# One statistics instruction for two tiles read in turns, and the variance made by GpSimd, in a six-layer attention and expert kernel

## The reference

```python
def _layernorm(x, w, b):
    m = jnp.mean(x, axis=-1, keepdims=True)
    v = jnp.mean(jnp.square(x - m), axis=-1, keepdims=True)
    return (x - m) * jax.lax.rsqrt(v + LN_EPS) * w + b
...
for i in range(DEPTH):                       # 6 layers
    xn = _layernorm(x, ln1_w[i], ln1_b[i])
    q, k, v = ...                            # xn @ wq, wk, wv, 8 heads of 16
    attn = _linear_attn(q, k, v)             # softmax of q over features, of k over tokens
    x = attn @ wo[i] + bo[i] + x
    xn = _layernorm(x, ln2_w[i], ln2_b[i])
    hdn = xn @ w1[i]                         # 128 -> 512
    hdn = jnp.where(hdn >= 0, hdn, LEAKY_SLOPE * hdn)
    x = hdn @ w2[i] + x                      # 512 -> 128
```

## Time and profile before

| | |
|---|---|
| time, median of 3 runs | 596.95 us (596.15 to 597.39) |
| span of the profiled execution, first to last instruction | 594.9 us |
| median of the runs less that span | 2.05 us |
| TensorE busy | 578.7 us (97%) |
| VectorE busy | 540.1 us (91%) |
| ScalarE busy | 434.8 us (73%) |
| GpSimd busy | 311.1 us (52%) |
| mean granted clock of TensorE | 0.994 of full speed |

### The profile page before, as it was taken

How to read it: one execution, slowest core, us unless ns; L and a number is a source line. 1 busy time by engine, 2 the same in 40 slices (tenths; PEclk the granted TensorE clock), 3 DMA queues, 4 the chain that set the end, 5 groups by cost and what they waited for, 6 DMA issues and landing times.

```text
span 594.9 us, 12614 instructions
## 1 busy us (share of the span) xinstructions
PE 578.7 (97%) x4166; PEld 516.3 (87%) x4166; DVE 540.1 (91%) x1352; ACT 434.8 (73%) x763; POOL 311.1 (52%) x308
## 2 busy tenths in 40 slices
PE   7999999999999999999999999999999999999897
PEld 7899897887978889889889898898898898898796
DVE  6887999999988999999999999999999999988865
ACT  2658595876976868868768768768779678687652
POOL 5896134755852772442442532433523766867752
PEclk9989999999999999999999999999999999999999
DMA  8209233323224154445435435445342351441102
GB/s 282 75 10 328 72 110 121 124 94 130 95 84 152 71 152 146 112 133 169 124 123 163 109 141 150 116 163 158 103 165 80 108 167 57 129 156 62 45 36 106
DMA packets 74946, 73.20 MB, mean 123 GB/s; under 512 B 27265, under 2 KB 65153, under 8 KB 74882
## 3 DMA queue, kind: packets, MB, share of 16 engines
q1 hardware_dynamic: 72400, 68.18, 35.6%
q0 software_dynamic: 2048, 4.20, 2.3%
q10 hardware_dynamic: 434, 0.02, 0.0%
HBM read 39.87 MB, written 32.51 MB: 122 GB/s over the span
## 4 chain that ended last, share of the span: by engine, by line
PE 75%; DVE 11%; DMA 4%; issue 3%; POOL 3%; ACT 2%; SPq 1%; DVEq 0%; ACTq 0%; POOLq 0%
PE psY L513 23%; PE psH L406 6%; PE psS L558 6%; PE psH L407 6%; PE psH L408 6%; PE psT L592 6%; PE psT L401 6%; PE psT L526 5%; PE psM L538 5%; DVE st L1295 2%; PE psS L455 2%; DMA through<-blocks 1%; DVE X L1563 1%; DVE hid L1553 1%; DMA turned<-through 1%
## 5 line engine op out<-in xcount | busy, mean ns | idle before, releaser
L513 PE MATMUL psY<-w_all,hid 128*128 128x128 f32 x1536 | 188.7, 276 | 2.5 <-DVE hid L1553 1.8
L513 PEld LDWEIGHTS psY<-w_all,hid 128*128 128x128 f32 x1536 | 182.0, 193 | 6.6 <-issue 2.3
L1553 DVE TENSOR_TENSOR hid<-psH,hsl 128x512 f32<-128x512 f32 x192 | 127.2, 676 | 13.6 <-ACT hsl L936 13.1
L936 ACT ACTIVATE hsl<-psH 128x512 f32<-128x512 f32 x192 | 108.3, 591 | 42.0 <-PE psH L408 38.5
L2038 POOL TENSOR_TENSOR rstd<-veps,minus_half 128x8 f32<-128x8 f32 x44 | 72.7, 1653 | 61.2 <-DVE veps L1312 61.0
L2134 POOL TENSOR_TENSOR qsm<-qe,qrec 128x1024 f32<-128x1024 f32 x24 | 46.5, 1938 | 97.8 <-DVE qrec L1636 97.8
L2112 POOL TENSOR_TENSOR xn_lo<-xn,xn_hi 128x512 fp32r<-128x512 f32 x48 | 60.6, 1282 | 69.4 <-ACT xn_hi L1000 69.4
L406 PE MATMUL psH<-xn_hi,w_hi 128*128 128x512 f32 x192 | 86.4, 450 | 3.7 <-DVE hid L1553 3.4
L966 ACT ACTIVATE xh<-X,shift,rstd 128x128 f32<-128x128 f32 x188 | 77.0, 482 | 8.9 <-POOL shift L2041 8.7
L408 PE MATMUL psH<-xn_lo,w_hi 128*128 128x512 f32 x192 | 76.1, 396 | 0.0
L407 PE MATMUL psH<-xn_hi,w_lo 128*128 128x512 f32 x192 | 76.0, 396 | 0.0
(11 more groups left out here) (161 smaller groups left out, 1024.9 us busy)
## 6 DMA issues: line engine op xcount, KB each, us to landing
through<-turn SPq DMA_DIRECT2D x22, 512.0 KB, 2.7
turn<-through SPq DMA_DIRECT2D x88, 128.0 KB
through<-blocks SPq DMA_DIRECT2D x20, 512.0 KB, 3.2
turned<-through SPq DMA_DIRECT2D x80, 128.0 KB, 2.8
wb<-expert_rows SPq DMA_DIRECT2D x40, 128.0 KB, 2.0
sorted_x<-blocks SPq DMA_DIRECT2D x5, 512.0 KB, 4.4
xs_xsT<-sorted_x SPq DMA_DIRECT2D x40, 64.0 KB, 2.5
sorted_y<-ys SPq DMA_DIRECT2D x10, 256.0 KB, 2.4
```

Source lines behind the costliest of these rows:

```text
L513: last = nc.tensor.matmul(tile(psY, t), tile(hid[:, c, :], t), w2_all[:, n // NBATCH, c, :], start=(c == 0 and t == 0), stop=(c == NC - 1) ...
L936: nc.scalar.activation(hsl[:, i % 2, :], psH[:, i % 2, :], ACT.Copy, scale=SLOPE) \
L1553: nc.vector.tensor_tensor(hid[:, i % NC, :], psH[:, i % 2, :], hsl[:, i % 2, :], ALU.max) \
```

## The change

Two neighbouring tiles are read by one statistics instruction, element 0 of the first, element 0 of the second, element 1 of the first, and so on. The even places are then the first tile and the odd places the second, so the six numbers are already the statistics of two whole tiles. Nothing is left to join. There are four statistics instructions of 256 columns for a norm in place of eight of 128. The seven small VectorE instructions of a norm go; GpSimd makes variance plus epsilon and the negated mean with two instructions of its own ahead of the power. For the input the nine small VectorE instructions become three, which stay on VectorE. statistics1 and statistics2 now wait, ahead of their first statistics, until the shift of the norm before is made, since GpSimd reads st.

```diff
-        st = sb("st", [P, NORMS, NT, 6])
-        sdiff = sb("sdiff", [P, NORMS, NT])
-        sdev = sb("sdev", [P, NORMS, NT])
+        st = sb("st", [P, NORMS, NT // 2, 6])
...
+        def two_in_turn(a):
+            return a.rearrange("p (t d) -> p d t", t=2)
+
+        def by_tile_of_pair(norm):
+            return st[:, norm, :, :].rearrange("p a (k f) -> p (a k) f", f=3)
+
+        def tile_means(norm):
+            return by_tile_of_pair(norm)[:, :, 1]
+
+        def tile_squares(norm):
+            return by_tile_of_pair(norm)[:, :, 2]
...
-            def tile_statistics(norm, name, src, tiles=range(NT)):
-
-                for t in tiles:
-                    last = nc.vector.bn_stats(st[:, norm, t, :], src(t))
-                last.then_inc(sig(name + "_st"), 1)
-
-            def token_statistics(norm, name, st_count, count):
...
+            def pair_statistics(norm, src, b, pairs):
+
+                for k in pairs:
+                    last = nc.vector.bn_stats(st[:, norm, k, :], two_in_turn(xb(src, b, 2 * k * P, 2 * P)))
+                return last
...
-                for t in range(NT):
-                    last = nc.vector.bn_stats(st[:, k, t, :], xb(xraw, b, t * P, P))
-                last.then_inc(sig("in_st"), 1)
+                pair_statistics(k, xraw, b, range(NT // 2)).then_inc(sig("in_st"), 1)
                 dve.wait_ge(sig("in_st"), b + 1)
...
+                nc.vector.tensor_scalar(both_var[:, b, :], tile_squares(k), (1.0 + EPS) / D, EPS * EPS,
+                                        ALU.mult, ALU.add)
+                nc.vector.tensor_scalar(negmean[:, k, :], tile_means(k), -1.0, None, ALU.mult)
+                nc.vector.tensor_scalar(veps[:, k, :], tile_squares(k), 1.0 / D, EPS, ALU.mult, ALU.add) \
+                    .then_inc(sig("in_var"), 1)
...
                     dve.wait_ge(sig("x1_added"), n + 1)
-                    tile_statistics(1, "ln2", lambda t: xb(X, n % NBATCH, t * P, P))
                     wait(dve, "ln2_shift", n)
-                    token_statistics(1, "ln2", n + 1, n + 1)
+                    pair_statistics(1, X, n % NBATCH, range(NT // 2)).then_inc(sig("ln2_st"), 1)
...
                     wait(dve, "y_added", 2 * (n - NBATCH) + half + 1)
-                    norm1_half(n % NBATCH, half)
...
+                    wait(dve, "ln1_shift", turned_before1(n))
+                    pair_statistics(0, X, n % NBATCH, range(2 * half, 2 * half + 2)).then_inc(sig("ln1_st"), 1)
...
-            def reciprocal_deviations(norm, name, count):
-
+            def reciprocal_deviations(norm, name, count, st_count):
+
+                pool.wait_ge(sig(name + "_st"), st_count)
+                nc.gpsimd.tensor_scalar(veps[:, norm, :], tile_squares(norm), 1.0 / D, EPS, ALU.mult, ALU.add) \
+                    .then_inc(sig(name + "_var"), 1)
+                nc.gpsimd.tensor_scalar(negmean[:, norm, :], tile_means(norm), -1.0, 1.0, ALU.mult, ALU.mult) \
+                    .then_inc(sig(name + "_mean"), 1)
                 pool.wait_ge(sig(name + "_var"), count)
                 nc.gpsimd.tensor_tensor(rstd[:, norm, :], veps[:, norm, :], minus_half[:, :], ALU.pow) \
                     .then_inc(sig(name + "_rstd"), 1)
+                pool.wait_ge(sig(name + "_mean"), count)
                 pool.wait_ge(sig(name + "_rstd"), count)
```

More of the change, by code:

```diff
@@ L1494, in expert_bias @@
                                         ALU.add).then_inc(sig("ys_ready"), 1)
-            def norm1_half(batch, half):
-                tile_statistics(0, "ln1", lambda t: xb(X, batch, t * P, P), range(4 * half, 4 * half + 4))
             def stage_w1(l):
@@ L1577, in statistics1 @@
                     wait(dve, "y_added", 2 * (n - NBATCH) + half + 1)
-                    norm1_half(n % NBATCH, half)
-            def variances1(n):
-                if there(n) and n >= NBATCH:
-                    k = turned_before1(n)
-                    wait(dve, "ln1_shift", k)
-                    token_statistics(0, "ln1", 2 * k + 2, k + 1)
+                    wait(dve, "ln1_shift", turned_before1(n))
+                    pair_statistics(0, X, n % NBATCH, range(2 * half, 2 * half + 2)).then_inc(sig("ln1_st"), 1)
             def blocks_of_norm1(n):
@@ L1754, in _ @@
             output_bias(3)
-            variances1(4)
             blocks_of_norm2(2)
@@ L1780, in _ @@
             leaky(2, 0)
-            variances1(5)
             leaky(2, 1)
@@ L1807, in _ @@
             value_bias(5)
-            variances1(6)
             leaky(3, 2)
@@ L1835, in _ @@
             statistics1(7, 1)
-            variances1(7)
             leaky(4, 0)
@@ L1856, in _ @@
             statistics1(8, 1)
-            variances1(8)
             add_attention(6)
@@ L1885, in _ @@
             leaky(6, 0)
-            variances1(9)
             leaky(6, 1)
@@ L1915, in slot @@
                 leaky(s - 3, 0)
-                variances1(s)
                 key_maxima(s - 1)
@@ L2118, in deviations2 @@
                     wait(pool, "xh2_ready", 4 * n)
-                    reciprocal_deviations(1, "ln2", n + 1)
+                    reciprocal_deviations(1, "ln2", n + 1, n + 1)
             def deviations1(n):
@@ L2126, in deviations1 @@
                         pool.wait_ge(sig("xh1_ready"), xh1_parts(n - 1))
-                    reciprocal_deviations(0, "ln1", k + 1)
+                    reciprocal_deviations(0, "ln1", k + 1, 2 * k + 2)
             def scale_queries(n):
```

28 lines of the change are left out of this document (removed).

## The result

The changed kernel took 592.72 us (median; 592.33 to 593.05) where the kernel before took 597.1 beside it: ratio 0.9926, 95% interval 0.9913 to 0.9939. Two further series on the same day gave 0.9936 (0.9902 to 0.9969) and 0.9964 (0.9944 to 0.9983). The mean of the three ratios, 0.9942, is 3.5 us. The profiled execution took 592.57 with a span of 590.8, 4.1 us shorter than the 594.9 before.

What follows compares the result with a forecast made beforehand. TensorE bounds the kernel, so freed VectorE time pays only where VectorE ends TensorE's wait behind statistics. Terms -1.0 - 1.9 - 3.4 + 0.4 = -5.9 us gave 591.0 us; range 585.6 to 596.0, the forecast's own 587.5 to 593.5.

Steps and rivals of the forecast that it cites:

- Prices: Unit costs: 412 ns for a 256-column statistics instruction, 0.2 us for each small GpSimd one; VectorE busy near 475 us.
- The rival of dear reading: Reading two tiles in turns takes 0.6 us a statistics instruction, so the kernel takes around 593.2 us; chance 0.08.
- Start: Input norms: statistics finish 1.1 us sooner, and TensorE's 1.04 us hole at 11.74 closes; -1.0 us.
- Middle: TensorE's holes at 94.79, 171.87 and 202.17, 2.9 us together, close by two thirds; -1.9 us.
- Regular middle: Regular slots gain nothing, since TensorE is busy for 20.00 of 20 us there; 0.
- Gather slots: Slots 21 to 23: GpSimd is the late engine and its added instructions lengthen the chain, about 0.15 us each; +0.4 us.
- the last sentence of the prediction: Signs of being wrong, among them xnT coming later in the gather slots by more than some tenths of a us.
- End: Last norm2: hid starts 3.3 us earlier, closing the 1.76 us hole and removing 1.64 us of clock loss; -3.4 us.
- Its sign, hid within 1.5 us of the first statistics: Check at the end: hid of the last norm2 starts within 1.5 us of that norm's first statistics.
- The holes move: TensorE meets the next late producer each time, leaving a small gain, 593.5 to 595.7 us; chance 0.13.
- Slower through GpSimd: Gather slots: GpSimd's two additions at 1.65 us each would make +12, 609 us; chance 0.07.

Runs made afterwards that it cites:

- more on GpSimd: Changed kernel with four further 8-column tensor_scalars a norm on GpSimd, into an unread buffer: 603.37 us, ratio 1.0131 to the kernel before.
- small ones on VectorE: Changed kernel, but VectorE makes the layer norms' variance plus epsilon and negated mean: 591.71 us, ratio 0.9913 to before; second run 592.12, 0.9938.

## Why the prediction was right, and by how much it was off

The direction and the place of the gains held; the forecast was 1.7 us below the first median, and the gain forecast (5.9) is above the 3.5 of three series. The median lies in the forecast's range, and part of how near it came is luck: the first series' four runs of the changed kernel lost 0.3 us each to low clock, those of the two later series 1.7 and 1.8. With the low-clock windows taken out, and the two executions of before against the three of the changed kernel, the table gives it term by term.

*Prices.* Right: 418 ns and 202 ns. Four statistics take 1.43 us, not 1.32, which was four steps of 0.33; three steps and the full length of the last, as the eight were counted, make 1.40. VectorE's busy time is 487.5 where 475 was forecast, 52.6 saved instead of 65; 4.8 of the difference are those 0.11 us in 44 norms, the rest wasn't traced. The rival of dear reading falls. The Trainium skill's figure for a source that hops at every element (page "Vector Engine (DVE) Microarchitecture Reference", section "Measured stream behaviour on trn2") would give some 590 ns, an estimate; the measured 418 ns contradict it for a statistics instruction over two tiles in turns. What the same section of the Trainium skill says of a one-source stream that alternates between regions, full rate, agrees with the 418 ns.

*Start, -1.0.* Right: 0.3 at number 67 and 0.9 more up to 301, 1.2. The hole is gone, both_shift starts at 8.29 (8.2 forecast), and VectorE's first normalised half at 8.77. But TensorE was still in its warm-up matmuls until 11.43 (11.03 and 12.15 in the other two executions), where the kernel before had ended them at 10.59 and 11.21, so most of the gain shows behind them. The hole's size is no fixed quantity either: 1.04 in one execution of the kernel before, 0.56 in the other.

*Middle, -1.9.* Right in sum: 180.6 to 178.5, 2.1. The hole at 94.79 went and one of 0.62 for xnT came 2.6 us behind it (in the third execution it is the other way round, 0.74 at 94.47 and none for xnT); 1.24 at 171.87 became 0.71; 0.94 at 202.17 went.

*Regular middle, 0.* Right in effect: 245.5 and 245.6 on average. It isn't the balance of a full TensorE, though: with xnT in time it takes 244.6. How often it doesn't come in time changes with the execution, in either kernel.

*Gather slots, +0.4.* Under-sized: 79.7 to 80.6, +0.8. These slots begin earlier by the lead and run into xnT, as the last sentence of the prediction has it. GpSimd's own share can't be told apart from the scatter here.

*End, -3.4.* The step that failed, in both its parts. (Its sign, hid within 1.5 us of the first statistics, failed too: it took 2.8, 1.37 of them waiting for ScalarE, but that was early enough for the hole to close.) "With the hole gone I expect most of the clock loss gone as well", 1.64 us, fell with the second execution of the kernel before (same hole, no window) and with the means of all runs, 1.3 us lost before and 1.5 after. And the 1.76 came out, 17.52 to 15.58, but with it the normalising instructions came 5 us earlier (564.14, once 569.18) and met GpSimd's addition: 1.08 lost. The prediction saw that GpSimd's power would come late there and called it covered; it looked for the instructions behind it in the queue of VectorE, not at what would run on GpSimd beside them. By the means of the executions that makes -1.9 and +1.1, -0.8 in all.

Sum: -1.2 - 2.1 + 0.1 + 0.8 - 0.8 = -3.2 us, near the 3.5 of the ratios.

*The rivals.* "The holes move" described the middle's mechanism rightly: TensorE does meet the next late producer, which there is mostly xnT. "Slower through GpSimd" was far off at 202 ns an instruction, but its price was too low: it counted the three gather slots alone. By it, 0.64 us a norm would be 3 x 2 x 0.64 = 3.8 us, near the 3.5 of the gather slots in "more on GpSimd"; in all it was 9.3, as the first slots wait as well. The sum gave the two small instructions +0.4 in the gather slots; by the two runs of "small ones on VectorE" the move to GpSimd costs 1.3, 0.6 of it at the end.

## What to carry to other kernels

A freed engine's time is worth only what the next late producer lets through: before trusting a gain, follow that producer's chain to something that the change shortens, or find that nothing does. The same trace reads differently for more work than for less: 52 us fewer on VectorE brought 3.5, about as many more, in the same place, cost 10 to 12, and 28 more on GpSimd cost 9, both with ScalarE waiting some 18 and 13 us longer for shift. Of a change in two parts each part wants its own run: here the move to GpSimd costs 1.3 us of what the paired statistics bring. And when an edit starts an instruction earlier, read what the engine that shares its path is doing at the new time, and take from no single execution a clock window as a property of the program: the mean clock of many runs tells what the windows are worth.

## What the runs showed of the hardware

- One-input VectorE instructions wait too. The first normalising tensor_scalar at 564.14 (128 columns, one tensor from SBUF) took 1,783 ns, 334 in the others, and ended at 565.92, 0.08 behind GpSimd's addition. In all nine executions in which it met that addition it took 1,165 to 2,385 ns and ended 0.08 to 0.09 behind it; where it didn't, 336 to 339. A negated mean of 8 columns (L1313) took up to 1,890: in the second run of "small ones on VectorE" 20 of the 44 took over 400 ns, and 19 of these end 0.02 to 0.04 us behind an addition or product of GpSimd. So the engines don't meet only in semaphores. The prediction had taken only instructions with two SBUF inputs for this kind. The Trainium skill (page "SBUF — State Buffer", section "SBUF: two separate sides") names, beside two SBUF inputs, VectorE's two-port mode as one that takes the pair shared with GpSimd and blocks until the other is through; the trace agrees in the end times, 565.92 and 565.84. Whether a tensor_scalar here runs in that mode no row shows. No statistics instruction was lengthened so: their mean is 418 or 419 ns in every kernel that has them, and the longest of the changed kernel's took 443.
- Low-clock windows of 3.4 us at 0.50 (the lower level, 1.2 GHz) come and go between executions of one kernel: at 35.6 and 564.7 or none for the kernel before, none, three or one for the changed; in "more on GpSimd" there is one of 6.8 us at 56.2. Apart from the one at 564.7 and some behind the last matmuls, those seen lie in the first 65 us.
- The 64 warm-up matmuls on the identity took 8.56 to 10.12 us in fourteen executions. The windows of the profile show a granted clock of 1.00 for all of it, but the matmuls don't agree: they start every 0.213 us at first and every 0.109 later. In the kernel before the pace doubles at 4.86 us, in its second execution at 6.13; in the three of the changed kernel at 6.57, 5.75 and 8.04, and each trace's clock record begins there. So the start, too, has a half-pace stretch whose length differs by execution, and it is what moves the start of number 67.
